# A GRU over 200 steps: who fetches its projected rows. ScalarE takes one block per turn, SyncE the final one

## The reference

```python
x = emb[item_seq]
mask = item_seq != 0
def step(h, inp):
    x_t, m_t = inp
    mx = x_t @ W + b_i
    mh = h @ U + b_r
    z = sigmoid(mx[:, :D] + mh[:, :D])
    r = sigmoid(mx[:, D:2*D] + mh[:, D:2*D])
    hh = tanh(mx[:, 2*D:] + r * mh[:, 2*D:])
    h_new = z * h + (1.0 - z) * hh
    h = where(m_t[:, None], h_new, h)
# 200 steps, then
softmax(h_last @ Wout + bout)
```

## Time and profile before

| | |
|---|---|
| median of 3 runs | 1032.23 us (1031.71 to 1033.38) |
| the profiled execution's own time | 1031.99 us |
| its span in the trace | 1030.2 us |
| PE busy | 976.1 us (95%) |
| DVE busy | 791.7 us (77%) |
| POOL busy | 762.5 us (74%) |
| ACT busy | 592.1 us (57%) |
| granted PE clock | 1.00 from 50 us on |

### The profile page before, as it was taken

How to read it: one execution, slowest core, us unless ns; L and a number is a source line. 1 busy time by engine, 2 the same in 40 slices (tenths; PEclk the granted TensorE clock), 3 DMA queues, 4 the chain that set the end, 5 groups by cost and what they waited for, 6 DMA issues and landing times.

```text
span 1030.2 us, 20749 instructions
## 1 busy us (share of the span) xinstructions
PE 976.1 (95%) x5218; PEld 756.3 (73%) x5218; DVE 791.7 (77%) x2075; ACT 592.1 (57%) x1301; POOL 762.5 (74%) x805
## 2 busy tenths in 40 slices
PE   6999999999999999999999999998989898899887
PEld 4556888777777777777777777776766666676665
DVE  3444667888888888888888888887777787787777
ACT  2334555666666666666666666665555555555555
POOL 5677777777777777777777777777777777777774
PEclk9999999999999999999999999999999999999999
DMA  9997555555555555555555555555555555555553
GB/s 356 402 372 289 148 162 162 165 160 164 160 162 162 161 163 160 162 162 161 164 160 162 162 161 163 160 162 162 160 163 161 161 161 162 164 162 163 161 158 109
DMA packets 62686, 184.74 MB, mean 179 GB/s; under 512 B 16767, under 2 KB 20538, under 8 KB 62602
## 3 DMA queue, kind: packets, MB, share of 16 engines
q0 software_dynamic: 48448, 147.18, 50.4%
q1 hardware_dynamic: 12758, 35.83, 9.1%
q10 hardware_dynamic: 1396, 0.91, 0.3%
HBM read 157.78 MB, written 26.07 MB: 178 GB/s over the span
## 4 chain that ended last, share of the span: by engine, by line
PE 59%; POOL 25%; issue 9%; DMA 3%; DVE 2%; ACT 1%; DVEq 0%; SPq 0%; POOLq 0%; ACTq 0%
POOL arena L376 25%; PE bank L470 15%; PE bank L476 10%; PE bank L472 10%; PE bank L458 9%; PE bank L392 5%; PE bank L464 4%; DMA rows<-arena 2%; PE bank L439 1%; PE bank L440 1%; PE bank L444 1%; DVE rh L642 1%; DVE h L647 1%; PE bank L397 1%; PE bank L432 1%
## 5 line engine op out<-in xcount | busy, mean ns | idle before, releaser
L376 POOL DMA_INDIRECT arena<-table,row_table x731 | 691.4, 946 | 222.9 <-issue 218.3
L576 ACT ACTIVATE bank<-bank,b_gates 128x256 f32<-128x256 f32 x400 | 179.5, 449 | 252.0 <-PE bank L476 252.0
L470 PE MATMUL bank<-h,U_sb 128*128 128x256 f32 x800 | 267.8, 416 | 4.3 <-DVE h L647 3.9
L657 DVE SCALAR_TENSOR_TENSOR bank<-bank,cand 128x256 f32<-128x256 f32 x400 | 172.9, 432 | 124.0 <-ACT cand L578 117.9
L458 PE MATMUL bank<-ident,arena 128*128 128x128 f32 x1496 | 229.9, 276 | 32.0 <-DMA arena<-table,row_table 31.2
L578 ACT ACTIVATE cand<-pre,bi 128x256 f32<-128x256 f32 x400 | 202.9, 507 | 89.2 <-DVE pre L651 89.0
L458 PEld LDWEIGHTS bank<-ident,arena 128*128 128x128 f32 x1496 | 179.1, 141 | 98.0 <-DMA arena<-table,row_table 70.5
L476 PE MATMUL bank<-h,U_sb 128*128 128x256 f32 x800 | 240.3, 382 | 0.0
L472 PE MATMUL bank<-h,U_sb 128*128 128x256 f32 x800 | 237.9, 379 | 0.0
L642 DVE SCALAR_TENSOR_TENSOR rh<-bank,br,r 128x256 f32<-128x256 f32 x400 | 193.6, 484 | 50.1 <-ACT r L574 47.1
L574 ACT ACTIVATE r<-bank,b_gates 128x256 f32<-128x256 f32 x400 | 190.0, 475 | 26.5 <-PE bank L470 23.1
(11 more groups left out here) (61 smaller groups left out, 250.2 us busy)
## 6 DMA issues: line engine op xcount, KB each, us to landing
arena<-table SPq DMA_DIRECT2D x2176, 1.5 KB
table<-arena SPq DMA_DIRECT2D x24, 768.0 KB, 5.1
arena<-table,row_table POOLq DMA_INDIRECT x731, 3.2
arena<-in_L_rec_emb SPq DMA_DIRECT2D x12, 512.0 KB, 10.1
rows<-arena SPq DMA_DIRECT2D x12, 512.0 KB, 10.3
raw<-rows,row_table POOLq DMA_INDIRECT x52, 4.7
seq<-in_r_item_seq ACTq DMA_DIRECT2D x1, 400.0 KB, 10.4
table<-arena SPq DMA_DIRECT2D x2, 192.0 KB
```

The lines of the kernel that those rows point to most:

```text
L376: pool.indirect_dma_start(ring_rows(s, k), None, table, bass.IndirectOffsetOnAxis(row_table[:, t, k:k + 1], 0)).then_inc(s_slot[s][c], 16)
L470: pe.matmul(reset_sum[c], U_sb[:, D:2 * D], h[c][:, :], start=False, stop=True, skip_group_check=True).then_inc(s_reset[c], 1)
L576: act.activation(update_sum[c], update_sum[c], ACT.Sigmoid, bias=b_gates[:, 0:1]).then_inc(s_z[c], 1)
L657: dve.scalar_tensor_tensor(out=update_sum[c], in0=update_sum[c], scalar=1.0, in1=cand[c][:, :], op0=ALU.subtract, op1=ALU.mult).then_inc(s ...
```

## The change

Four edits.

1. Block 3 of slot 0 (`ACT_SLOT`) is fetched by ACT from the second turn on, in the way SP does it: 8 blocks, 128 rows each. The rows are spread over the steps 1 to 19 of the turn ahead, 7 per step (2 in the last). A step has one `TENSOR_LOAD` of its 7 offsets behind the r of chain 0, and the row DMAs stand behind ACT's six activations as `BEHIND` says: 0, 1, 1, 3, 1, 1.
2. SP's loop is written with a hint that prefetches the loop's head, as the loops of the other engines are.
3. Block 3 of the very last step (`LAST_BLOCK`) is fetched by SP, after its last block of before.
4. U, Wout and bout are loaded in the middle of the projection, not at the start.

POOL's list is 9 gathers shorter, 722 in place of 731. The offsets need more columns, which costs POOL two small instructions during setup, SP a third DMA to `slow_line`, and DVE one small memset.

```diff
+LAST_BLOCK = 3
+ACT_SLOT = (0, 3)
...
+    BEHIND = (0, 1, 1, 3, 1, 1)
+    AT_ONCE = sum(BEHIND)
...
             for b in range(len(SLOW)):
-
-                sp.dma_start(slow_line[b:b + 1, 0:(TURNS + 1 - b) * P],
-                             slow_turned[b * (TURNS + 1):2 * TURNS + 1 if b else TURNS + 1, :]
+                sp.dma_start(slow_line[b:b + 1, :], slow_turned[b * (TURNS + 1):(b + 1) * (TURNS + 1), :]
                              ).then_inc(s_slow_line, 16)
+            sp.dma_start(slow_line[2:3, P:(TURNS + 1) * P], slow_turned[2 * TURNS + 2:3 * TURNS + 2, :]
+                         ).then_inc(s_slow_line, 16)
...
-            with sp.Fori(1, TURNS) as turn:
+            with nc.Fori(1, TURNS, engines=[sp.engine], hint_back_edge=True) as turn:
                 for b in range(len(SLOW)):
                     slow_block(b, turn)
             slow_block(0, TURNS)
+            for first in range(0, P, BATCH_ROWS):
+                offset = load_offsets(sp, 1, TURNS, first, BATCH_ROWS)
+                if first == 0:
+                    sp.wait_ge(s_free[1], (TURNS - 1) * RING + LEFT)
+                for i in range(BATCH_ROWS):
+                    sp.dma_start(ring_rows(LEFT - 1, LAST_BLOCK)[first + i:first + i + 1, :].bitcast(U8),
+                                 table_bytes[:, bass.ds(offset[i], ROW_BYTES)]).then_inc(s_last_block, 16)
...
                     for k in CHAINS[c]:
-                        if (s, k) in SLOW:
+                        if (s, k) in SLOW or (s, k) == ACT_SLOT and n >= RING or (t, k) == (STEPS - 1, LAST_BLOCK):
                             continue
...
+                if last:
+                    pe.wait_ge(s_last_block, P * 16)
...
+                        elif n == 0 and (s, k) == ACT_SLOT:
+                            pe.wait_ge(s_act_rows, turn * (P * 16) + 1)
...
-            for dst, src in ((U_sb, U), (bi, b_i), (br, b_r), (Wout_sb, Wout), (bout_sb, bout.partition_broadcast(P))):
+            for dst, src in ((bi, b_i), (br, b_r)):
...
             for i in range(CHUNKS, PIECES, 2):
+                if i == 2 * CHUNKS + AHEAD:
+
+                    for dst, src in ((U_sb, U), (Wout_sb, Wout), (bout_sb, bout.partition_broadcast(P))):
+                        act.dma_start(dst[:, :], src).then_inc(s_params, 16)
                 copy_proj(i)
...
+                    first = (s - ACT_SLOT[0] - 1) * AT_ONCE
+                    n = min(AT_ONCE, P - first) if steps == RING and first >= 0 else 0
+
+                    def fetch(place):
+                        for p in range(sum(BEHIND[:place]), min(sum(BEHIND[:place + 1]), n)):
+                            fetch_row(act, 2, first + p, offset[p]).then_inc(s_act_rows, 16)
+
                     for c in BOTH:
-                        gates(t, c)
-
+                        reset(t, c)
+                        if n > 0 and c == 0:
+                            offset = load_offsets(act, 2, turn + 1, first, n)
+                            if first == 0:
+                                act.wait_ge(s_free[1], turn * RING + ACT_SLOT[0] + 1)
+                        fetch(3 * c)
+                        update(t, c)
+                        fetch(3 * c + 1)
+                        candidate(t, c)
+                        fetch(3 * c + 2)
```

More of the change, by code:

```diff
@@ L52, in gru @@
     LEFT = STEPS - RAW - TURNS * RING
-    assert SLOW[0][0] < LEFT <= SLOW[1][0]
+    assert ACT_SLOT[0] < SLOW[0][0] < LEFT <= SLOW[1][0]
+    BEHIND = (0, 1, 1, 3, 1, 1)
+    AT_ONCE = sum(BEHIND)
+    assert ACT_SLOT[0] + P // AT_ONCE + 1 < RING
     BOTH = range(len(CHAINS))
@@ L115, in gru @@
         row_table = sb("row_table", [P, STEPS, BLOCKS], I32)
-        slow_offsets = sb("slow_offsets", [P, 2 * TURNS + 1])
-        slow_turned = sb("slow_turned", [2 * TURNS + 1, P], I32)
-        slow_line = sb("slow_line", [len(SLOW), (TURNS + 1) * P], I32)
+        slow_offsets = sb("slow_offsets", [P, 3 * TURNS + 2])
+        slow_turned = sb("slow_turned", [3 * TURNS + 2, P], I32)
+        slow_line = sb("slow_line", [len(SLOW) + 1, (TURNS + 1) * P], I32)
         copy_i = sb("copy_i", [P, 1], I32)
@@ L184, in gru @@
         s_slow_line = sem("slow_offsets_on_one_partition")
+        s_act_rows = sem("act_rows_fetched")
+        s_last_block = sem("last_block_fetched")
         s_slow = [sem(f"slow{b}_rows_fetched") for b in range(len(SLOW))]
@@ L225, in fetch_row @@
         def fetch_row(eng, b, p, offset):
-            return eng.dma_start(ring_rows(*SLOW[b])[p:p + 1, :].bitcast(U8),
+            return eng.dma_start(ring_rows(*(SLOW + (ACT_SLOT,))[b])[p:p + 1, :].bitcast(U8),
                                  table_bytes[:, bass.ds(offset, ROW_BYTES)])
@@ L277, in _ @@
             sp.wait_ge(s_padrow, 16 * 2)
-            sp.wait_ge(s_slow_line, 16 * len(SLOW))
+            sp.wait_ge(s_slow_line, 16 * (len(SLOW) + 1))
             def slow_block(b, turn):
@@ L345, in _ @@
                                    ).then_inc(s_offsets, 1)
+            pool.tensor_scalar(slow_offsets[:, 2 * TURNS + 1:2 * TURNS + 2],
+                               row_f[:, LAST_BLOCK, STEPS - 1:STEPS], float(ROW_BYTES), None, ALU.mult
+                               ).then_inc(s_offsets, 1)
+            pool.tensor_scalar(slow_offsets[:, 2 * TURNS + 2:3 * TURNS + 2],
+                               row_f[:, ACT_SLOT[1], RAW + ACT_SLOT[0] + RING:STEPS:RING], float(ROW_BYTES), None,
+                               ALU.mult).then_inc(s_offsets, 1)
             pool.tensor_copy(row_table[:, :, :], row_f.rearrange("p k t -> p t k")).then_inc(s_idx, 1)
             pool.wait_ge(s_idx, 8)
-            pool.wait_ge(s_offsets, len(SLOW))
+            pool.wait_ge(s_offsets, len(SLOW) + 2)
             pool.wait_ge(s_pins, 2)
@@ L419, in _ @@
                 project(i)
-            slow_bank = bank[1][0:2 * TURNS + 1, 0:P]
-            pe.wait_ge(s_offsets, len(SLOW))
+            slow_bank = bank[1][0:3 * TURNS + 2, 0:P]
+            pe.wait_ge(s_offsets, len(SLOW) + 2)
             pe.wait_ge(s_tdve, CHUNKS + 1)
@@ L450, in transpose_rows @@
             def transpose_rows(turn, s, c):
-                gathered = sum((s, k) not in SLOW for k in CHAINS[c])
-                pe.wait_ge(s_slot[s][c], (turn + 1) * (16 * gathered) + (32 if s < RAW else 0))
+                gathered = sum((s, k) not in SLOW + (ACT_SLOT,) for k in CHAINS[c])
+                more = (32 if s < RAW else 0) + sum(16 for k in CHAINS[c] if (s, k) == ACT_SLOT)
+                last = isinstance(turn, int) and (turn, s) == (TURNS, LEFT - 1) and LAST_BLOCK in CHAINS[c]
+                pe.wait_ge(s_slot[s][c], (turn + 1) * (16 * gathered) + more - (16 if last else 0))
+                if last:
+                    pe.wait_ge(s_last_block, P * 16)
                 for i, k in enumerate(CHAINS[c]):
@@ L570, in turned_x, with reset, update, candidate @@
                 act.copy(xT[c][:, :], x_sum[c]).then_inc(s_xT[c], 1)
-            def gates(t, c):
+            def reset(t, c):
                 act.wait_ge(s_reset[c], t + 1)
                 act.activation(r[c][:, :], reset_sum[c], ACT.Sigmoid, bias=b_gates[:, 1:2]).then_inc(s_r[c], 1)
+            def update(t, c):
                 act.wait_ge(s_update[c], t + 1)
                 act.activation(update_sum[c], update_sum[c], ACT.Sigmoid, bias=b_gates[:, 0:1]).then_inc(s_z[c], 1)
+            def candidate(t, c):
                 act.wait_ge(s_pre[c], t + 1)
                 act.activation(cand[c][:, :], pre[c][:, :], ACT.Tanh, bias=bi[:, 2:3]).then_inc(s_tanh[c], 1)
+            def gates(t, c):
+                reset(t, c)
+                update(t, c)
+                candidate(t, c)
             for t in range(RAW):
@@ L590, in one_turn @@
                     t = RAW + turn * RING + s
-                    for c in BOTH:
-                        gates(t, c)
+                    first = (s - ACT_SLOT[0] - 1) * AT_ONCE
[3 more added lines that the diff above has]
+                            fetch_row(act, 2, first + p, offset[p]).then_inc(s_act_rows, 16)
+                    for c in BOTH:
+                        reset(t, c)
+                        if n > 0 and c == 0:
[3 more added lines that the diff above has]
+                        fetch(3 * c)
+                        update(t, c)
+                        fetch(3 * c + 1)
+                        candidate(t, c)
+                        fetch(3 * c + 2)
+            act.wait_ge(s_slow_line, 16 * (len(SLOW) + 1))
+            for q in range(AHEAD):
+                act.wait_ge(s_store[q], 16 * table_stores(q))
+            act.wait_ge(s_padrow, 16 * 2)
             over_table_steps(act, one_turn)
@@ L603, in _ @@
         def _(dve):
+            dve.memset(inv_total[:, :], 0.0).then_inc(s_act_rows, 1)
             dve.memset(pad_raw[:, :], 0.0).then_inc(s_const, 1)
@@ L632, in _ @@
             dve.wait_ge(s_slow_turned, 1)
-            dve.tensor_copy(slow_turned[:, :], bank[1][0:2 * TURNS + 1, 0:P]).then_inc(s_slow_copied, 1)
```

(1 more changed line is left out.)

## The result

The changed kernel takes 1078.36 us (median of 4, 1077.37 to 1079.97), the kernel before 1032.17 beside it: ratio 1.045, 95% interval 1.0438 to 1.0463. It is 46.2 us slower, so the forecast of 1025 us, 0.7% faster, was wrong in sign. The range, 1019 to 1056, does not hold it either.

What follows compares the result with a forecast made beforehand. It took the recurrence to bound the first stage and POOL's gathers the second. PE going on at 1020.9 - 8.1 + 1 = 1013.8 us gave a span of 1023.1, plus 1.8 around it: 1025 us, range 1019 to 1056.

Steps and rivals of the forecast that it cites:

- the load's price: ACT's register load of 7 offsets behind chain 0's r: taken as 0.9 us, between 0.45 and 2.04.
- Even 1.3 us would be harmless: ACT's load between r and z: 1.3 us costs nothing, since z's result has 0.3 us before DVE's product.
- Rival D: ACT itself is late, by a 2.04 us load or DMAs waiting for activations: 1107 us, half effect 1054; chance 0.17.
- POOL: right within 2 us: POOL's gather queue: nine gathers fewer save 11.3 us and the start 0.4, last gather landing at 1009.2 us.
- The start: Moving U, Wout and bout away from the start: frees 0 to 1.8 us, taken as 0.4.
- SP: the right engine, 8 us too early: SP's final block sets the new end, landing at 1012.8 us, 3.6 us behind POOL's last gather.
- the six passes of the loop: SP's loop with the hint: six returns at 0.3 us instead of 3.1 give 16.8 us back.
- the landing: SP's last row: lands 1.9 us after issue, taken from the output's landing.
- Contention: SP and ACT issuing DMAs at once: bounds 0 and 0.05 us per ACT DMA, taken as 1 ns, 1 us in all.
- rival A: SP's final block ends last, as summed, with up to 5 ns per ACT DMA: 1021 to 1030 us, chance 0.50.
- rival C: ACT's DMAs hold up SP's, slower from 9 ns per DMA on; body 1035 to 1060 us, chance 0.20.
- Rival E: One DMA engine is full, at 88%, so rows land later: 1027 to 1040 us, chance 0.05.

Runs made afterwards that it cites:

- e5: Kernel before, plus 38 register loads of 1 to 32 offsets from starts 0 to 20 on ACT in its eighth turn, values used; 1038.74 us.
- e9: Changed kernel, but each ACT load takes 12 offsets from a multiple of four and 7 are used; 1033.37 us, ratio 0.9972.
- e6: Changed kernel with 8 rows per step, loads at multiples of 8, and the final block left to POOL; 1020.8 us, ratio 0.9889.
- e8: Kernel before with only U, Wout and bout loaded later, in the middle of the projection; 1030.61 us, ratio 0.9988.
- e3: Changed kernel with 8 rows a step, so every load takes eight offsets from a multiple of eight; 1033.3 us, ratio 0.9998.
- e4: Changed kernel without ACT's row fetch, POOL gathering slot 0 again, the other three edits kept; 1030.49 us, ratio 0.9988.
- e2: Changed kernel with ACT's 7 offsets loaded once ahead of the turns, all 1024 row DMAs kept; 1034.53 us, ratio 1.0016.

## Why the prediction was wrong

**The step that failed: the load's price.** "Its price for 7 offsets isn't in the trace: 32 offsets take 2.04 us. Between 7/32 of this, 0.45, and all of it, 2.04, I take 0.9." What was measured is 1.14 us when the load begins at a multiple of four and 1.72 when it doesn't (e5). Seven rows a step make the loads begin at 0, 7, 14, 21, 28 and so on, so of a turn's 19 loads 5 are short, 13 long, and the last one, of two offsets, small (0.66). Over eight turns that is 8 steps at +0.23, 32 at +0.13 and 104 at +0.67, 76 us in all. The recurrence had 32.3 us to spare; 76 less 32 is 44 us, and 46.2 were measured. That the price of the load is the cause doesn't rest on this sum: e9 changes it alone, and 45 us come back. The one row of a load in the trace before was of 32 offsets from a multiple of four, the cheapest form there is, so its share per offset was no guide to seven.

**"Even 1.3 us would be harmless" failed with it.** The load starts 0.08 us after r starts, and z starts 0.05 after the load ends (0.10 and 0.17 for the first load of a turn). So of the 1.09 us between r and z 0.96 are open to a load, and e9's loads of 0.96 just fit. The slack of 0.3 that z's result has before DVE's product is not the one that counts: the first DMA behind z takes 0.47 us, where the prediction had 0.32 for a row, and the tanh starts behind it, 0.60 after z, 0.67 before. That leaves 0.07, so that a load of 1.15, with z 0.18 late, already costs 0.13 a step.

**Rival D was the right mechanism.** It had ACT late by the load, at 2.04 us and 0.7 a step, 1107 us, or half of it, 0.35, 1054. Measured were 1.72 us for most loads and 0.50 a step as a mean over 152 steps. Its chance of 0.17 was too small for a price that was open between 0.45 and 2.04, with a decision at 0.16 us a step: the middle of those bounds, 1.25, was already past the window of 1.09 us.

**POOL: right within 2 us.** With nine gathers fewer and an earlier start PE was to go on at 1009.2. e6 leaves POOL one gather more, which makes the same sum 1010.5, and has 1009.4. The start gained 1.2 us (e8), not 0.4.

**SP: the right engine, 8 us too early.** With the load's price mended (e3, e9), SP's final block does end last, as forecast, but PE goes on at 1021.5 and not 1013.8. Of these 7.7 us the six passes of the loop are 3.7 (625.0 us before and 611.9 in e4, so 13.1 saved and not 16.8; a return of 0.7 us in place of 0.3 accounts for 2.4 of it), the way from the loop's end to the final block, with the stall, 2.3, the ACT DMAs 2.4 (3.4, not 1), and the landing -0.5 (1.4, not 1.9). That is 7.9, 0.2 too much. Then the tail is 1.6 us longer, at the lower clock. 1025 + 7.7 + 1.6 = 1034.3; e3's profiled execution took 1034.25. So even with a cheap load, the final block on SP gives away all that POOL gains. Left with POOL, it is worth 12.5 us (1033.3 to 1020.8), and 10.4 with loads of twelve (1033.4 to 1022.9).

**Contention: small, though more than taken.** 3.3 to 3.9 ns per ACT DMA (e3, e2 and e9 against e4) where 1 was put in, within rival A's 5, far from rival C's 9 ns and from the bound of 50. By the rule of the Trainium skill that the prediction cited (Perfetto Trace Analysis, DMA Instruction — HWDGE), a lock held for a whole issue would cost up to 0.2 us each; the runs show a fiftieth of it. Rival E had nothing in the runs: the last row landed in 1.38 us.

**Open.** In the kernels that end with SP's block and have ACT DMAs (e2, e3, e9), 4 of 30 executions took 1020.8 to 1023.6 us, some 11 us less than the others. None of them was profiled, so what goes otherwise there isn't known; e4, without ACT DMAs, had no such execution in ten. Their granted clock over the whole execution is 0.993 to 0.996, that of the other 26 is 0.987 to 0.995, which would fit a PE that doesn't stand idle before the last step, and shows no more than that. Nor do the runs show why SP stalls behind its loop or where the last 2 us of the 46 lie.

## What to carry to other kernels

Price an instruction by its form, not by its share of a larger one: one row of 32 offsets said nothing about seven, and most of the loads of seven were priced wrong by a factor of two, in 152 steps of a recurrence. Load offsets in fours from a multiple of four, even if some aren't used. A queue that ends last with PE idle before it costs its lateness and the lower clock that PE then starts with, so the last piece of work belongs to the queue that would finish it first, which isn't the one that is free first: in e6 SP is free at 970.5 us but needs 48 for the block, POOL takes it in one gather of 1.25.

## What the runs showed of the hardware

- A register load on ACT (e5): about 0.26 us and 0.24 for each four offsets from a multiple of four, and about 0.2 for each offset that is in no such four. Eight take 0.72 us, seven 1.14 or 1.72.
- The first row DMA on ACT behind such a load takes 0.47 us, later ones 0.23 (the change; in e2, with one load in all, they take 0.23 as a median).
- A loop whose head is hinted returns in 0.7 us on SP (e4), 3.1 without; some 15 us after leaving the hinted loop, SP stalled once for about 2.7 us.
- PE, idle for 12.2 us (e3), began again at a granted clock of 0.50, and four transposes took 1.09 us instead of 0.66.
